# Causal attention beside its own next group: one more empty place behind each block's split in the side items

## The reference, cut to what matters

```python
qkv = einsum('bsi,oi->bso', x, w_qkv); q, k, v = split(qkv, 3)      # 16 heads of 8
logits = einsum('bhsd,bhtd->bhst', q, k) / sqrt(8)
logits = where(tril, logits, -inf)
probs = softmax(logits, axis=-1)
out = einsum('bhst,bhtd->bhsd', probs, v) ... ; return einsum('bsi,oi->bso', out, w_out)
# then: x = x + attention(layernorm(x)); then a six-layer stack with local attention
# and a gated FFN, grouped attention, and the same stack once more
```

## Time and profile before

| | us |
|---|---|
| median of 3 runs | 6230.59 |
| lowest, highest | 6227.81, 6245.38 |
| the profiled execution, its own time | 6235.06 |
| its span in the trace | 6233.3 |
| PE busy in it | 5654.6 (91%) |
| DVE, ACT, POOL busy | 4598.0, 3397.3, 4338.2 |
| TensorE's granted clock, mean | 0.971 of 2.4 GHz |

### The profile page before, as it was taken

One profiled execution on the slowest core, in us unless ns is written; L12 is line 12 of the kernel. 1 busy time (PEld: TensorE's weight loads), 2 busy tenths in 40 slices (PEclk: granted clock), 3 DMA queues, 4 the chain that ended last, 5 costly groups with the idle time before them and its releaser, 6 DMA issues. The chain is left out here.

```text
span 6233.3 us, 177427 instructions
## 1 busy us (share of the span) xinstructions
PE 5654.6 (91%) x76063; PEld 3916.3 (63%) x76063; DVE 4598.0 (74%) x6111; ACT 3397.3 (55%) x4021; POOL 4338.2 (70%) x2126
## 2 busy tenths in 40 slices
PE   7888979888989998899999999999788999999898
PEld 4444457767777777565555555554476777777675
DVE  6555469998989998675556555552598888888896
ACT  1444656666766666334444444434466666666664
POOL 2000069888888888327777777779788888888884
PEclk7999989999999999999999999999899999999999
DMA  0000022222222222100000000000122222222221
GB/s 26 2 2 2 12 57 67 71 74 66 71 71 74 64 70 62 35 1 1 1 1 1 1 1 1 1 1 12 42 63 77 62 76 68 72 69 68 63 69 49
DMA packets 188209, 253.46 MB, mean 41 GB/s; under 512 B 60829, under 2 KB 81817, under 8 KB 187289
## 3 DMA queue, kind: packets, MB, share of 16 engines
q1 hardware_dynamic: 187416, 242.03, 15.0%
HBM read 38.98 MB, written 1.57 MB: 7 GB/s over the span
## 5 line engine op out<-in xcount | busy, mean ns | idle before, releaser
L2140 POOL TENSOR_TENSOR XB<-XB,Pb 128x1024 f32<-128x1024 f32 x448 | 1072.4, 2394 | 340.1 <-ACT Pb L2098 299.4
L933 POOL TENSOR_TENSOR sin_qk<-raw_qk,rot 128x512 f32<-128x512 f32 x768 | 1000.1, 1323 | 25.8 <-ACT raw_qk L885 25.6
L2155 DVE TENSOR_REDUCE b_pmax<-slot 128x1 f32<-128x512 f32 x1024 | 653.0, 682 | 326.0 <-PE slot L1885 324.8
L2098 ACT ACTIVATE Pb<-slot 128x1024 f32<-128x1024 f32 x512 | 503.6, 1024 | 709.7 <-PE slot L1996 671.3
L949 POOL TENSOR_TENSOR rot_out<-rot_out,sin_qk 128x1024 f32<-128x1024 f32 x192 | 629.0, 3276 | 366.6 <-DVE rot_out L1012 365.9
L966 POOL TENSOR_TENSOR inv_norm<-norm2c,minus_half 128x16 f32<-128x16 f32 x192 | 685.7, 3571 | 32.6 <-DVE norm2c L1113 17.2
L538 PE MATMUL slot<-w_hi,x_hi 128*128 128x512 f32 x1152 | 551.5, 479 | 62.9 <-DVE rot_out L1012 45.1
L958 POOL TENSOR_TENSOR inv_norm<-norm2c,minus_half 128x16 f32<-128x16 f32 x192 | 558.8, 2910 | 55.8 <-DVE norm2c L1060 54.1
L803 ACT ACTIVATE V<-slot 128x1024 f32<-128x1024 f32 x192 | 196.6, 1024 | 577.4 <-PE slot L540 577.4
L2008 PE MATMUL slot<-Pb,Vb 128*64 128x512 f32 x2048 | 499.0, 608 | 9.8 <-DVE b_inv L2202 8.7
L1016 DVE TENSOR_TENSOR rot_out<-rot_out,inv_norm 128x1024 f32<-128x1024 f32 x384 | 478.9, 1247 | 6.5 <-POOL inv_norm L958 5.9
(11 more groups left out here) (213 smaller groups left out, 13217.9 us busy)
## 6 DMA issues: line engine op xcount, KB each, us to landing
VW<-V SPq DMA_DIRECT2D x1152, 128.0 KB, 2.4
VW<-V SPq DMA_DIRECT2D x768, 64.0 KB, 2.1
w_raw<-in_Wqkv SPq DMA_DIRECT2D x36, 512.0 KB, 3.7
Wo<-in_Wo SPq DMA_DIRECT2D x12, 512.0 KB, 4.2
W<-in_W SPq DMA_DIRECT2D x12, 341.0 KB, 3.2
consts<-in_shape_constants SPq DMA_DIRECT2D x1, 2436.5 KB, 9.2
QH<-rows_dram SPq DMA_DIRECT2D x128, 2.0 KB
QB<-rows_dram SPq DMA_DIRECT2D x128, 2.0 KB
```

The costliest lines, as they stand in the source:

```text
L933: ins = pool.tensor_tensor(dst[:, :, x, :], src[:, :, 1 - x, :], tab, ALU.mult)
L2098: act.activation(Pb[:, at % B_RING, :], slot[n % 2][:, :], ACT.Exp).then_inc(s["b_exp"], 1)
L2140: pool.tensor_tensor(b_sum[:, window % 2, :], Pb[:, (at - 1) % B_RING, :] if k == 1 else b_sum[:, window % 2, :], Pb[:, at % B_RING, :], A ...
L2155: dve.tensor_reduce(b_pmax[:, n // 2, u:u + 1], o[:, 512 * x:512 * x + 512], AX.X, ALU.max)\
```

## The change

One `("rest",)` more stands behind each `("split", b)` in the list, so a group has 182 entries where it had 178. For block 0 it comes ahead of `("v",)`, for blocks 1 to 3 ahead of the first tile of maxima.

```diff
         A_ITEMS = []
         for b_ in range(NB):
-            A_ITEMS += [("qk", b_), ("rest",), ("rest",), ("split", b_)]
+            A_ITEMS += [("qk", b_), ("rest",), ("rest",), ("split", b_), ("rest",)]
             if b_ == 0:
                 A_ITEMS += [("v",), ("rest",)]
             if b_:
```

## The result

Over 20 runs the changed kernel takes 6227.82 us (median; 6223.47 to 6240.02), the kernel before 6233.68 us (6224.37 to 6248.02). The ratio is 0.9987 with a 95% interval of 0.9981 to 0.9993, that is 8 us faster, between 4 and 12. The forecast was 11.5 us.

What follows compares the result with a forecast made beforehand. PE's order was taken as the path, with about 20 us idle a round to win. 2.3 + 0 + 2.4 + 4.8 - 1.0 + 3.0 = 11.5 us gained from the median 6230.59 gives 6219 us, range 6204 to 6238.

Steps and rivals of the forecast that it cites:

- rival A: The gain comes as summed: 6219 us, between 6213 and 6226; chance 0.55.
- v: Half of the next unit's scores moves ahead of v; gap 3.7 to 3.3 us; 2.3 us gained, bounds 1.2 and 2.3.
- Block 1: Values and sums go ahead of qk, at the lower clock; taken as 0, bounds 2 us either way a round.
- Block 2: Longer chain, tile 7.4 us behind qk; idle 1.7 instead of 2.33 us; 2.4 us gained, bounds 0 and 4.
- Block 3: qk behind both halves of scores; idle 1.4 instead of 2.33 us; 4.8 us gained, bounds 2 and 7.
- Tiles: More places hold two entries; one more wait of 0.3 us a round costs 1.0 us, bounds 0 and 3.
- The clock: Half of four low-clock stretches, at block 2's gaps and qk, go; 3 us gained, bounds 0 and 6.8.
- The page's rule: Frequent short idle gaps between matmul groups make the clock swing; by it the clock term is zero, the sum 8.5 us.
- Rival B: The clock holds: low stretches at block 2 go, those at v and block 1 shorten; 6205, fully 6196 us; chance 0.15.
- Rival C: The waits only move, to tiles and other places, and the clock swings as before; 6228 us (6226 to 6233); chance 0.18.
- Rival D: Slower: the clock stays low behind v until behind block 1's first tile; 6239 us; chance 0.12.
- the signs: Among others: PE's waits for KT's split fall from 20.5 to 15 us or less, qk's for tiles below 1 us a round.

Runs made afterwards that it cites:

- e6: The change with three more empty places ahead of v and two each behind the splits of blocks 1 to 3 (188 entries); ratio 0.9963 to the kernel before.
- e5: The change with three more empty places ahead of v (185 entries); ratio 0.9965 to the kernel before.
- e1: The kernel before with the empty place behind block 0's split only (179 entries); 6257.37 us, executed once, beside 6261.14 us before.
- e8: The change with five empty places ahead of v and three behind the other splits (192 entries); ratio 0.9952 to the kernel before.

## Why the prediction was right, point by point

- *The size.* 11.5 us were forecast, the mark shows 10.4 and the times show 8 and 11. The mechanism of rival A came, at v and at blocks 2 and 3. That the sum fits so well is partly luck: the tiles took some 2.5 us more than forecast and the clock gave some 2.5 us more.
- *v.* The gap was to be 3.3 and is 3.16; the half of scores took 0.77 behind v and now runs ahead of it. The gap is as forecast; the 2.3 us for it were not measured by themselves.
- *Block 1*, taken as 0 with 2 us either way. Its gap, forecast at 2.1 at the full clock, is 3.00, 1.28 and 1.47 in the three rounds, where it was 2.94, 1.89 and 1.60. The low stretch behind the tile, 6.3 us at 0.50, is gone in the second and third rounds of all three profiles of the change, but the stretch at v is longer by as much, and the two together hold 44 to 51 us in either kernel. So 0 was a fair value.
- *Block 2.* Tile at 7.4, measured 7.6; gap 1.7, measured 1.83; wait of qk 0.6, measured 0.51. A gain of 0.8 us a round, as forecast.
- *Block 3.* Tile at 6.2, measured 6.21; gap 1.4, measured 1.22; wait of qk 0.2, measured 0.27. 1.6 us a round, as forecast.
- *Tiles.* Forecast at 0.3 us a round, measured at 0.7, 1.1 and 0.9 in the three rounds and another 0.3 in each at the turns: 3.6 us in all, where I had 1.0 and an upper bound of 3. The step that failed is the count of places with two tiles: e6 has more of them with only 6.2 us of waits.
- *The clock.* Forecast at 3.0 us with bounds 0 and 6.8, measured at some 5.5, in sum all of it at blocks 2 and 3, where I had put it. I counted four such stretches and took half of them to go; one is left. It made good what the tiles took.
- *The page's rule*, that short gaps alone make the clock swing (the Trainium skill, "TensorE: Matmul & The Clock Gate", section "A second HAM failure mode: psum-queue depth-cycling"), is borne out in the direction: smaller gaps of 1 to 2 us left 11 us less at the lower clock. It did not hold to the letter. The gap of 1.83 us in block 2 was followed by a low stretch in the second round of each profile of the change and in no other round, and those of about 1.2 us in block 3 by none.
- *Rival B*, a chance of 0.15, did not come with this change at v. e5 shows that its mechanism is real, in part, once v's gap is 1 us. *Rival C* came in part, at the tiles. *Rival D* came in part, and its sign appeared: the clock was to come back later than 12 us behind v's start, and it comes back 16.5 us behind it (343.8 to 360.3), where it was 12.5 before. Values, sums and qk all run low, as D has it. But D's price needed it to stay low up to block 1's tile, and it is back 2.4 us ahead of it; the window behind that tile stands at 1.00.
- *The range* of 6204 to 6238 holds 6227.82. Of the signs, the waits for the split fell to 15.0 us, as asked; the waits of qk are 1.1 us a round, not below 1. I had named as a sign of being wrong that the stages behind 790 us differ by more than a few us. In the profiled executions the stack does, by 10.7 us, and why stays open.

## What to carry to other kernels

Where an item waits for a buffer that a chain of other engines gives back, write down the chain's length from its start and the work placed between, for each place separately: at v and at blocks 2 and 3 the gaps of the change and of e1 were foretold within 0.2 us, while the count of empty places told nothing. Block 1's gap, and those of e8, were not foretold so well. An entry added to an evenly dealt list moves everything behind it, and whether a step lands ahead of or behind a neighbour on ACT or DVE (7.6 against 6.2 us here) is worth more than the entry itself. Look at the granted clock behind each gap as well: in e5, with v's gap down to 1 us and block 2's to 0.9, the rounds lost another 18 us, twice what the whole change had brought, and about half of that goes with 17 us less at the lower clock.

## What the runs showed of the hardware

- v, 16 float32 products of 32 columns, took 7.04 us behind a gap of 3.2 us in the second and third rounds of the kernel after, all of it at 1.2 GHz, and 4.43 to 6.17 us behind a gap of 1.0 us in e5. With PE busy all through, the clock did not rise during v in any round, and it fell during v where v had begun at 2.4 GHz. That was so in the first round of both kernels too, within 1 us, behind gaps of 3.7 and 3.2 us.
- From v's start on (343.8 to 360.3 us of the kernel after) PE was busy for 16.5 of 16.5 us and the granted clock stayed at 0.50.
- The same gap of 2.33 us (2.42 in one case) was followed by the lower clock behind block 2 in all three rounds of the first profile of the kernel before and behind block 3 in none; in the other two profiles of before, block 3's was followed by it once each, at 244 and 247 us.
- Executions of one kernel begin the first round up to 7 us apart (157.3 to 164.7 us with the change), and then take 643.8 to 645.6 us for the rounds.
